# Scaling the output weights pair by pair on GpSimd, and adding the projection's bias on TensorE, in a pre-norm attention and expert-layer kernel

## The reference

```python
def _L0_attn_ref(x, Wqkv, bqkv, Wout, bout, rel_k_emb, rel_v_emb, alphas_raw):
    q, k, v = (to_heads(t) for t in split(x @ Wqkv.T + bqkv))
    scores = einsum('bhid,bhjd->bhij', q, k) * SCALE + einsum('bhid,ijd->bhij', q, rel_k)
    threshold = top_k(scores, 32)[0][..., -1:]
    attn = softmax(where(scores < threshold, -inf, scores))
    alphas = sigmoid(alphas_raw)
    res, v_curr = 0, v
    for i in range(ORDER):                        # ORDER = 3
        a_v = attn @ v_curr  (+ attn @ rel_v for i == 0)
        v_curr = a_v
        res = res + alphas[i][None, :, None, None] * v_curr
    return res.transpose(0, 2, 1, 3).reshape(b, n, INNER) @ Wout.T + bout
x = x + attention(layernorm(x))
x = x + expert_layer(layernorm(x))
```

## Time and profile before

| | before |
|---|---|
| time, median of 3 runs | 726.46 us (726.28 to 728.13) |
| the profiled execution | 727.17 us |
| its span, first to last instruction | 725.4 us |
| busy share: DVE, PE, ACT, POOL | 94%, 91%, 85%, 74% |
| mean granted TensorE clock | 0.983 |

### The profile page before, as it was taken

The page is one execution under the profiler, slowest core; times in us unless marked ns, Lnnn a source line. Parts: engine busy times, 40 slices in busy tenths (PEclk is TensorE's granted clock), DMA queues, the critical chain, the costliest instruction groups (busy, mean ns, idle before and its releaser), DMA issues.

```text
span 725.4 us, 20794 instructions
## 1 busy us (share of the span) xinstructions
PE 656.9 (91%) x5736; PEld 511.6 (71%) x5736; DVE 684.4 (94%) x2841; ACT 619.4 (85%) x1754; POOL 535.1 (74%) x917
## 2 busy tenths in 40 slices
PE   4377989999999999999999999999999999998795
PEld 3255777777777777777777777777777777776574
DVE  5898989999999999999999999999999999999825
ACT  3668788989999899999999899999999899997843
POOL 1588888878887778878887778878887778777511
PEclk9779999999999999999999999999999999999998
DMA  6735444444545454554545454444545454453202
GB/s 196 191 108 147 132 121 146 136 146 137 150 138 152 125 160 129 153 150 133 149 132 151 131 161 139 143 146 137 149 132 157 127 159 140 143 149 110 63 21 59
DMA packets 148338, 98.72 MB, mean 136 GB/s; under 512 B 10624, under 2 KB 147968, under 8 KB 148096
## 3 DMA queue, kind: packets, MB, share of 16 engines
q1 hardware_dynamic: 147920, 97.32, 46.1%
q10 hardware_dynamic: 304, 0.08, 0.0%
HBM read 45.59 MB, written 51.77 MB: 134 GB/s over the span
## 4 chain that ended last, share of the span: by engine, by line
DVE 74%; issue 10%; POOL 6%; PE 5%; DMA 2%; ACT 2%; SPq 0%; ACTq 0%; POOLq 0%; DVEq 0%
DVE top L668 38%; DVE work L674 33%; POOL s_sb L322 3%; DMA band_scratch<-zeros 1%; DVE rinv L655 1%; POOL s_sb L297 1%; PE ps_p L888 1%; ACT a_sb L437 1%; POOL wk L365 1%; POOL x_sb L370 1%; PE ps_s L966 1%; PE ps_y L903 1%; PE ps_d L874 1%; ACT pen L427 1%; DVE stats L691 0%
## 5 line engine op out<-in xcount | busy, mean ns | idle before, releaser
L668 DVE MAX8 top<-work 128x8 f32<-128x256 f32 x768 | 285.3, 414 | 0.0
L674 DVE MATCH_REPLACE8 work<-top,work 128x256 f32<-128x256 f32 x512 | 206.4, 412 | 0.0
L322 POOL TENSOR_TENSOR s_sb<-s_sb,pen 128x512 f32<-128x512 f32 x127 | 162.0, 1276 | 59.6 <-ACT pen L427 59.6
L327 POOL TENSOR_SCALAR a_sb<-a_sb,rinv 128x256 f32<-128x256 f32 x254 | 119.3, 481 | 57.2 <-DVE rinv L655 56.6
L437 ACT ACTIVATE a_sb<-s_sb,nmax 128x256 f32<-128x256 f32 x256 | 128.1, 501 | 34.9 <-POOL s_sb L322 26.9
L427 ACT ACTIVATE pen<-s_sb,limit 128x256 f32<-128x256 f32 x254 | 116.4, 511 | 34.7 <-POOL limit L309 34.7
L297 POOL TENSOR_TENSOR s_sb<-s_sb,skew 128x384 f32<-128x384 f32 x128 | 128.4, 1003 | 2.7 <-DMA skew<-band_scratch 2.7
L888 PE MATMUL ps_p<-aT,rows 128*64 128x256 f32 x1024 | 125.1, 385 | 4.9 <-issue 3.3
L674 DVE MATCH_REPLACE8 work<-top,s_sb 128x256 f32<-128x256 f32 x256 | 103.1, 412 | 0.0
L888 PEld LDWEIGHTS ps_p<-aT,rows 128*64 128x64 f32 x1024 | 70.1, 136 | 41.8 <-issue 16.1
L668 DVE MAX8 top<-s_sb 128x8 f32<-128x256 f32 x256 | 94.6, 412 | 4.1 <-POOL s_sb L297 4.1
(11 more groups left out here) (135 smaller groups left out, 1285.0 us busy)
## 6 DMA issues: line engine op xcount, KB each, us to landing
skew<-band_scratch SPq DMA_DIRECT2D x128, 192.0 KB, 2.7
diag_scratch<-a_sb SPq DMA_DIRECT2D x128, 192.0 KB, 2.4
band_scratch<-band SPq DMA_DIRECT2D x128, 191.0 KB, 3.5
diag<-diag_scratch SPq DMA_DIRECT2D x128, 128.0 KB, 2.3
wqkv<-in_wqkv SPq DMA_DIRECT2D x1, 1152.0 KB, 7.7
x_sb<-in_x SPq DMA_DIRECT2D x4, 256.0 KB, 4.9
wout<-in_wout SPq DMA_DIRECT2D x1, 512.0 KB, 5.4
out<-xn SPq DMA_DIRECT2D x1, 512.0 KB, 3.3
```

The source lines that it names most:

```text
L322: nc.gpsimd.tensor_tensor(s_sb[g % 4][:], s_sb[g % 4][:], pen[g % 2][:], ALU.subtract).then_inc(pen_added, 1)
L327: nc.gpsimd.tensor_scalar(a_sb[g % 3][:, t, :], a_sb[g % 3][:, t, :], rinv[g % 2][:, t:t + 1], 1.0, ALU.mult, ALU.mult).then_inc(normed, 1)
L668: nc.vector.max(m[:, t, 8 * n:8 * n + 8], src).then_inc(top_step, 1)
L674: nc.vector.match_replace(work[t][:, n % 2, :], m[:, t, 8 * n:8 * n + 8], src, LOW).then_inc(top_step, 1)
```

## The change

GpSimd's three products of 128 by 1024 numbers behind slots 1 to 3 and its four additions of 128 by 512 numbers behind slots 4 to 7 go. In slots 1 to 8 `scale_wout(hp, a, e)` makes the blocks of pair hp = q - 1: two of them between `negative_max(2q + 1)` and `add_penalty(2q)`, the third between `add_skew(2q + 2)` and `normalise(2q)`. Each is a product of 128 by 128 numbers with one number per partition. `project(p)` waits for the blocks of its own pair only, and for the first pair of each sequence it begins with the product of the identity and `bout`, once for each of the two row blocks; all further products add to it. VectorE no longer waits for `xb_done`.

```diff
--- before.py
+++ after.py
@@ -136,7 +136,7 @@
             sem(n) for n in ("relk_in", "cols_in", "w_in", "w_in2", "late_in", "wout_in", "ffn_in"))
         made, scratch_zero = sem("made"), sem("scratch_zero")
         relk_done, cols_done, relv_done = sem("relk_done"), sem("cols_done"), sem("relv_done")
-        alpha_exp, alpha_done, wk_done, xb_done = sem("alpha_exp"), sem("alpha_done"), sem("wk_done"), sem("xb_done")
+        alpha_exp, alpha_done, wk_done = sem("alpha_exp"), sem("alpha_done"), sem("wk_done")
         dve_p, row_stats, var_done, std_done = sem("dve_p"), sem("row_stats"), sem("var_done"), sem("std_done")
         xn_done, xnT_ready, xnT_saved = sem("xn_done"), sem("xnT_ready"), sem("xnT_saved")
         qk_ready, qk_saved, q0_ready = sem("qk_ready"), sem("qk_saved"), sem("q0_ready")
@@ -335,6 +335,14 @@
                 src = bass.AP(aT[p % 4][:].tensor, MAXREL, [[2 * T * N, P], [T * N, 2], [N + MAXREL, T], [1, MAXREL]])
                 nc.gpsimd.tensor_tensor(clip[p % 2][:], src, mask[:], ALU.mult).then_inc(clipped, 1)
 
+            def scale_wout(hp, a, e):
+
+                pool.wait_ge(alpha_done, 1)
+                pool.wait_ge(wout_in, 16 * 2)
+                for i in range(a, e):
+                    nc.gpsimd.tensor_scalar(wk[:, i, hp, :], wout[:, hp, :], al[:, hp, i:i + 1], 1.0, ALU.mult,
+                                            ALU.mult).then_inc(wk_done, 1)
+
             def slot(q):
                 if on(q - 1):
                     scale_limit(2 * q - 1)
@@ -353,22 +361,16 @@
                 if on(q):
                     scale_limit(2 * q)
                     negative_max(2 * q + 1)
+                if 1 <= q <= NP:
+                    scale_wout(q - 1, 0, 2)
+                if on(q):
                     add_penalty(2 * q)
                 if on(q + 1):
                     add_skew(2 * q + 2)
+                if 1 <= q <= NP:
+                    scale_wout(q - 1, 2, ORDER)
                 if on(q):
                     normalise(2 * q)
-
-            def scale_wout(i):
-                pool.wait_ge(alpha_done, 1)
-                pool.wait_ge(wout_in, 16 * 2)
-                nc.gpsimd.tensor_tensor(wk[:, i, :, :], wout[:], al[:, :, i:i + 1].to_broadcast([P, NP, DIM]),
-                                        ALU.mult).then_inc(wk_done, 1)
-
-            def add_bout(g):
-                pool.wait_ge(xn_done, TILES)
-                nc.gpsimd.tensor_tensor(x_sb[:, 4 * g:4 * g + 4, :], x_sb[:, 4 * g:4 * g + 4, :],
-                                        bout[:].unsqueeze(1).to_broadcast([P, 4, DIM]), ALU.add).then_inc(xb_done, 1)
 
             def add_base(i, a, e):
 
@@ -380,10 +382,6 @@
 
             for q in range(-3, PAIRS - 1):
                 slot(q)
-                if 1 <= q <= ORDER:
-                    scale_wout(q - 1)
-                if ORDER < q <= ORDER + GROUPS:
-                    add_bout(q - ORDER - 1)
 
             q = PAIRS - 1
             scale_limit(2 * q - 1)
@@ -679,7 +677,6 @@
 
             def add_projection(b):
                 i = slice(T * b, T * (b + 1))
-                dve.wait_ge(xb_done, GROUPS)
                 dve.wait_ge(proj_done, NP * (b + 1))
                 nc.vector.tensor_tensor(y_sb[:, i, :], ps_y[:, 0:T * DIM].rearrange("p (t c) -> p t c", t=T), y_sb[:, i, :],
                                         ALU.add).then_inc(y_done, 1)
@@ -891,17 +888,19 @@
 
             def project(p):
                 b, hp = divmod(p, NP)
-                pe.wait_ge(wk_done, ORDER)
+                pe.wait_ge(wk_done, ORDER * min(p + 1, NP))
                 pe.wait_ge(r1_saved, 2 * p + 2)
                 pe.wait_ge(r2_saved, p + 1)
                 if hp == 0:
                     reach(pe, y_done, b)
+                    for t in range(T):
+                        mm(ps_y[:, t * DIM:(t + 1) * DIM], ident[:], bout[:], start=(t == 0), stop=False)
                 for i, r in enumerate((r1T[p % 3], r2T[p % 2], r3T[p % 2])):
                     if i == 2:
                         pe.wait_ge(r3_saved, p + 1)
                     for t in range(T):
                         last = mm(ps_y[:, t * DIM:(t + 1) * DIM], r[:, t * P:(t + 1) * P], wk[:, i, hp, :],
-                                  start=(hp == 0 and i == 0 and t == 0), stop=(hp == NP - 1 and i == ORDER - 1 and t == T - 1))
+                                  start=False, stop=(hp == NP - 1 and i == ORDER - 1 and t == T - 1))
                 last.then_inc(proj_done, 1)
 
             def second_power(p):
```

## The result

| | before | after |
|---|---|---|
| time, median | 727.3 us (726.28 to 728.93, 4 runs) | 716.97 us (716.14 to 719.82, 4 runs) |
| ratio, 95% interval | | 0.9869 (0.9853 to 0.9885) |
| the profiled execution | 727.17 us | 719.82 us |
| its span | 725.4 us | 718.1 us |
| busy share: DVE, PE, ACT, POOL | 94%, 91%, 85%, 74% | 95%, 92%, 86%, 74% |

The change is faster by 1.3%, 9.5 us by the ratio.

The account below looks back on a forecast made before the run. Bound: the loop normalise, limit, ramp, penalty, exponent, rinv, with GpSimd's large products paid nearly in full. 10.37 - 1.3 - 0.1 - 0.2 = 8.8 us less: 717.7 us from the median 726.46, 718.4 from the profiled execution; range 715.9 to 720.6.

Parts of the forecast that it names:

- The large products go, 10.37 us: GpSimd's products and additions behind slots 1 to 7 delay DVE's rinv; removing them gains 10.37 us if nothing takes their place.
- Three small products per slot, cost 0: GpSimd, slots 1 to 8: at 340 ns each, two fit ahead of the penalty, the third ahead of `normalise`; cost 0.
- The upper bound of 481 ns: At 481 ns per small product the pair ends 0.1 us too late for the penalty; eight slots cost 0.8 us.
- Slot 2, 1.3 us from TensorE's clock: TensorE at 1.2 GHz until 45 us makes bands and transposes late; rinv(3) loses 0.55 us, 1.3 us in all.
- Clean: Rival, chance 0.20: nothing is uncovered in slot 2, bands and transposes being in time; 716.3 us.
- The 0.1 us for save_xnT: Behind rinv(4), save_xnT makes ScalarE some 0.1 us late once more.
- The bias, 0.2 us: Two bias products on TensorE delay `save_rows` and the ramp; about 0.2 us in slot 4 alone, later sequences 0.
- slot 9 terms: Times given as in slot 9 of the trace before, which has neither the large products nor the bias.
- SP's queue and the drain are untouched: SP's transfer queue and the drain after the last pair were taken as unchanged, with no term in the sum.

Follow-up runs that it names:

- r0: The changed kernel once more, no edit; 717.65 us, ratio 0.9881 to the kernel before.
- r1: The change with GpSimd's four bias additions put back behind slots 4 to 7 and no bias on TensorE; 721.76 us, ratio 0.9938 to the kernel before.
- r3: The change with all three small products of a slot behind `normalise`, in the loop; 726.32 us, ratio 0.9981 to the kernel before.
- r11: The change with all three small products of a slot ahead of the penalty; 718.47 us, ratio 0.9881 to the kernel before.
- r4: The change with the four loads of `load_ffn` moved from slot 2 to slot 14; 718.66 us, ratio 0.9879 to the kernel before.
- r5: The change with 44 unused identity products keeping TensorE busy before slot 2; 717.27 us, ratio 0.9870 to the kernel before.
- r8: The change with SP's issues of skew and band put between a tile's send and its fetch; 717.09 us, ratio 0.9874 to the kernel before.
- r7: The change with `load_ffn` in slot 14, TensorE kept busy before slot 2 and the first bias in slot 3; 719.21 us, ratio 0.9879.
- r10: The kernel before, large products kept, with SP's skew and band issues between send and fetch; 726.97 us, ratio 1.0000.
- r2: The change with GpSimd's three large products put back behind slots 1 to 3, bias on TensorE; 722.0 us, ratio 0.9933 to the kernel before.
- r9: The change with SP's skew and band issues between send and fetch, TensorE busy before slot 2, first bias in slot 3; 715.91 us, ratio 0.9847.

## Why the prediction was right, and where it was not

The direction, the size and the range held: 717.7 us was said, 716.97 measured (717.65 in r0), range 715.9 to 720.6. The main term, the large products, carries this. That the number came so close is luck in part: the terms of 1 us behind it were missed in both directions and vary from execution to execution. Against its own profiled execution the sum gave 718.4, and that execution took 719.8. Step by step:

- **The large products go, 10.37 us.** Right. r1 and r3 show what is behind it from the other side: what stands behind `normalise` is paid nearly in full, 1.20 us of an addition of 1.27 and 1.0 us of 1.06.
- **Three small products per slot, cost 0.** Right, and close: 375 ns and not 340, 0.73 us for the pair in a gap of 0.82. r11's trace shows that 0.36 us more would not have fit, and r3 that the place is worth 5.6 us or more. The upper bound of 481 ns was not reached.
- **Slot 2, 1.3 us from TensorE's clock.** The mechanism is shown: by the band copies in the profile after, by save_aT in r4, and by r0, where the clock was back and the loss gone. Its size and its certainty were off. The clock came back at 39.7, 43.7 and 44.7 us in r0, the change and r4, so the loss is 0, 0.85 or 1.4 us. I took the time of the one trace of before as a fact about the kernel. The loss was absent in three of the seven profiles of the table at r0, so "Clean", the rival without it, deserved more than 0.20. (The row gives 45.92 for the end of L803, not 45.98.) The 0.1 us for save_xnT was not seen: the steps of tiles 5 to 7 are 5.03 to 5.04 us in the change.
- **The bias, 0.2 us.** 0.10 to 0.12 us in r5, r4 and r8, where TensorE comes in time, and 0.63 us at tiles 9 and 10 in both profiles of the change, where it comes late. The working in slot 9 terms was near for the first case; it assumed that TensorE is on time in slot 4.
- **"SP's queue and the drain are untouched."** This is the step that failed. No instruction of SP moved, but its cover did. In the slots of 11.9 and 11.3 us it could be behind without harm: from 50 to 125 us it waited 16.1 us for GpSimd. At 10.07 us, with two waits for a landing (send to fetch 2.7 to 4.5 us) and 1.9 us of issues of skew and band in each slot, these waits are gone, and the diagonals are late in slot 4. Tile 8 lost 0.91 us by it in one profile, 0.14 in the other. r7 and r8 show the chain; the waits of SP in the two traces show that the cover was there before.

The misses partly cancel: slot 2 lost 0.5 us less than said and slots 4 and 5 1.3 us more; tile 18 added 0.15 us; the drain was 1.0 us longer, with one more late start of the diagonals there (0.67 us of idle time, which r0 does not have), the start 0.5 us shorter. That is how this execution came out 1.4 us above its sum.

What stays open: the groups of runs 3 us apart, in r3 and in r8, were never met in a profile that can be set beside its other group. In r8 the upper group has the lower mean clock (0.978 and 0.979), in r5 the clock is the same in all runs, and in r3 it does not separate the groups (0.982 to 0.985 below, 0.978 to 0.984 above). So one cause is not enough, and what else it is, late transfers or something unseen, is not shown.

## What to carry to other kernels

When a loop's stages lose a stall that made all of them slow, go through every queue of those stages, the untouched ones too, and ask whether it can keep the new pace; its waits for the other engines in the old trace are the time it has to spare. A queue that waits for each transfer to land before its next issue is the first to look at. An engine's idle gap is a place for work only to the length of the wait that ends last in it, and the same work a few instructions on, behind the product that the loop waits for, costs its full length. A term that rests on when a clock or a transfer happened to come in one trace is a range, not a value.

## What was not expected of the hardware

- In executions in which TensorE does the same work up to slot 2, its clock, low since 26 to 29 us, returned to 2.4 GHz at very different times, from 38.9 (r10) and 39.7 (r0) over 43.7 (the change) to 45.0 (before) and 45.9 us (r2). In r2, r3 and r10 it fell once more within the first 65 us. Filling its idle time with products kept the clock up in r5 and r7, but in r9 it fell to 1.2 GHz at 40.2 us all the same, behind an idle time of TensorE of 2.0 us that r5 has as well. The Trainium skill, "TensorE: Matmul & The Clock Gate", section "What's actually happening", says that the point of the return varies from run to run, and gives half a microsecond to either side for it; the runs agree that it varies, but by 7 us here.
- From the send of 192 KB to the fetch that waits for it to land it was 2.04 us for the most part where the send stood ahead of skew and band (r8), and 2.6 to 4.9 us from 41 to 125 us where it stood behind them (the change and r0).
